# A graph-transformer layer on one core: experts' weight splits in smaller portions, own row buffers, aligned rows, and GpSimd subtracts every fourth piece

## The reference

```python
xn = _layernorm(x)
x = x + graph_layers(xn, src, dst) + linear_attention(xn)
xf = _layernorm(x)
probs = softmax(xf @ router_w);  topw, topi = top_k(probs, 2)
h = silu(einsum('nd,edf->nef', xf, w1))            # w1: 8 x 1024 x 1024
ye = einsum('nef,efd->ned', h, w2)                 # w2: 8 x 1024 x 1024
routed = einsum('ne,ned->nd', combine, ye)
shared = sigmoid(xf @ shared_gate_w) * ((silu(gate) * up) @ shared_down)
out = x + routed + shared
```

## Time and profile before

| | |
|---|---|
| median of 3 runs | 1055.58 us (1055.2 to 1055.6) |
| the profiled execution's own time | 1056.61 us |
| its span, first to last instruction | 1054.6 us |
| mean granted TensorE clock | 0.996 of full speed |
| PE busy | 1032.0 us (98%) |
| VectorE busy | 649.6 us (62%) |
| ScalarE busy | 459.5 us (44%) |
| GpSimd busy | 79.1 us (8%) |

### The profile page before, as it was taken

One profiled execution on the slowest core, in us unless ns is written; L12 is line 12 of the kernel. 1 busy time (PEld: TensorE's weight loads), 2 busy tenths in 40 slices (PEclk: granted clock), 3 DMA queues, 4 the chain that ended last, 5 costly groups with the idle time before them and its releaser, 6 DMA issues.

```text
span 1054.6 us, 16055 instructions
## 1 busy us (share of the span) xinstructions
PE 1032.0 (98%) x6128; PEld 908.3 (86%) x6128; DVE 649.6 (62%) x962; ACT 459.5 (44%) x731; POOL 79.1 (8%) x123
## 2 busy tenths in 40 slices
PE   7999999999999999999999999999999999999998
PEld 5889998787787899978878999988979788998977
DVE  6789968667655765324356362244867678776546
ACT  4413344547777423220232422223666566655440
POOL 6000010000000000000000035000100010000003
PEclk9999999999999999999999999999999999999999
DMA  9722112123321222341200544233886897686618
GB/s 354 303 80 73 49 41 80 41 80 128 101 70 41 81 80 81 136 158 64 80 1 1 178 151 96 100 131 130 282 299 235 310 315 237 252 297 227 240 38 294
DMA packets 76694, 156.44 MB, mean 148 GB/s; under 512 B 8489, under 2 KB 8987, under 8 KB 76618
## 3 DMA queue, kind: packets, MB, share of 16 engines
q1 hardware_dynamic: 65656, 127.30, 34.9%
q0 software_dynamic: 6416, 20.00, 5.5%
q10 hardware_dynamic: 4546, 8.10, 2.1%
HBM read 133.89 MB, written 21.49 MB: 147 GB/s over the span
## 4 chain that ended last, share of the span: by engine, by line
PE 82%; DVE 7%; ACT 4%; DVEq 2%; DMA 2%; issue 1%; POOL 1%; ACTq 0%; POOLq 0%; SPq 0%
PE ps L1982 20%; PE ps L1984 20%; PE ps L1983 20%; PE ps L2446 5%; PE ps L2447 2%; PE ps L2471 2%; DVE w_lo L1188 2%; PE ps L2081 1%; PE ps L2313 1%; PE ps L2314 1%; PE ps L2244 1%; PE ps L2245 1%; PE ps L2095 1%; DMA y_first<-expert_rows,slots 1%; PE ps L2472 1%
## 5 line engine op out<-in xcount | busy, mean ns | idle before, releaser
L1194 DVE TENSOR_TENSOR w_lo<-w_raw,w_hi 128x2048 fp32r<-128x2048 f32 x41 | 93.1, 2288 | 38.5 <-ACT w_hi L800 36.4
L2446 PE MATMUL ps<-xe,w_hi 128*128 128x304 f32 (+2 forms) x384 | 107.6, 356 | 0.0
L1982 PE MATMUL ps<-w_hi,xt_hi 128*128 128x512 f32 (+1 forms) x240 | 96.0, 400 | 3.9 <-DVEq L1504 2.0
L800 ACT CAST w_hi<-w_raw 128x2048 fp32r<-128x2048 f32 x41 | 77.1, 1908 | 45.1 <-PE ps L2314 36.2
L2447 PE MATMUL ps<-xe,w_lo 128*128 128x152 f32 (+2 forms) x384 | 94.8, 247 | 0.0
L1188 DVE TENSOR_TENSOR w_lo<-w_raw,w_hi 128x1024 fp32r<-128x1024 f32 x68 | 78.7, 1220 | 24.5 <-ACT w_hi L796 23.9
L1984 PE MATMUL ps<-w_hi,xt_lo 128*128 128x512 f32 (+1 forms) x240 | 93.7, 390 | 0.0
L1983 PE MATMUL ps<-w_lo,xt_hi 128*128 128x512 f32 (+1 forms) x240 | 93.5, 390 | 0.0
L1188 DVE TENSOR_TENSOR w_lo<-w_late,w_hi 128x1024 fp32r<-128x1024 f32 x64 | 74.1, 1219 | 20.4 <-ACT w_hi L796 19.2
L1982 PE MATMUL ps<-xt_hi,w_hi 128*128 128x314 f32 x256 | 79.4, 310 | 0.0
L1982 PE MATMUL ps<-t_hi,w_hi 128*128 128x314 f32 x256 | 78.8, 308 | 0.0
(11 more groups left out here) (371 smaller groups left out, 2375.8 us busy)
## 6 DMA issues: line engine op xcount, KB each, us to landing
w_raw<-in_L_ffn_w SPq DMA_DIRECT2D x64, 512.0 KB, 5.4
w_late<-in_L_ffn_w SPq DMA_DIRECT2D x64, 512.0 KB, 5.8
w_raw<-in_L_gnn_W_neigh SPq DMA_DIRECT2D x8, 1024.0 KB, 6.1
w_raw<-in_L_gnn_W_self SPq DMA_DIRECT2D x8, 1024.0 KB, 5.1
w_raw<-in_L_ffn_shared_gate_up SPq DMA_DIRECT2D x8, 1024.0 KB, 6.2
expert_rows<-ctx_s POOLq DMA_DIRECT2D x15, 512.0 KB, 13.3
w_raw<-in_L_mix_Wv SPq DMA_DIRECT2D x4, 1024.0 KB, 14.8
w_raw<-in_L_mix_Wk SPq DMA_DIRECT2D x4, 1024.0 KB, 5.3
```

Of the source, the lines that this page charges most:

```text
L800: copy(w_hi[b][:, s * HK:(s + 1) * HK, :], w_raw[s][:, :, :]).then_inc(hi_done, 1)
L1194: V_.tensor_tensor(w_lo[b][:, k, :], w_raw[s][:, :, :], as32(w_hi[b][:, k, :]), ALU.subtract).then_inc(lo_done, 1)
L1982: mat(out_ap, lh, rh, start=start, stop=False)
L2446: mat(PS(key)[:, a, 0:2 * width], wh[:, k, w_cols], xe[:, :, k, 0:width], start=k == 0, stop=False)
```

## The change

Four things at once.

1. **GpSimd subtracts.** The last of the four pieces of every job of the experts is subtracted by GpSimd (`last_lo`), in its queue between the gathers; DVE does three. It counts on a semaphore of its own, for which PE and SP wait (`wait_lo`). Each gather of the next expert's rows now stands behind the subtraction for the present expert's first job.
2. **Split portions.** ACT and DVE no longer do a whole job at a time while they make the hidden values: the first piece of a job goes ahead of the SiLU of units n = 1 and n = 3, the rest behind it. In a ONE expert the cast of job J+2 goes ahead of the rows of the expert before, and the transposes of the next expert's last tile go behind the first `y` unit. Turned outputs `yf` use two buffers in place of four; the reduction of `yf` 2 waits until the first two have been turned back.
3. **Own row buffers.** In a ONE expert, which has one tile of rows, the two halves go to two buffers in place of one.
4. **Aligned rows.** `BS` is 256, so that each block of `xe` and `he` is 1024 bytes; `at_hi` and `q_first` start 64 bytes lower. The late buffer of the fourth piece moves to a place that is free by then.

```diff
-    B, BS = 224, 224
+    B, BS = 224, 256
...
-            return [("ht", q, 0)] + following[:2] + [("ht", q, 1)] + following[2:] + y_units(q)
+            return [("ht", q, 0)] + following[:2] + [("ht", q, 1)] + y_units(q)[:1] + following[2:] + y_units(q)[1:]
...
-        at_hi = at("at_hi", RG, [128, KF, TQ], f32r)
+        at_hi = at("at_hi", RG - RG % 512, [128, KF, TQ], f32r)
...
+        row_buffer = lambda q, h, s: h if ONE[q] else s
...
+            def last_lo(job, base=None):
+
+                pool.wait_ge(hi_done, by(count_at(job, PARTS - 1), base, 4 * PARTS))
+                k = slice((PARTS - 1) * PK, PARTS * PK)
+                nc.gpsimd.tensor_tensor(w_lo[job % 2][:, k, :], raw_part(job, PARTS - 1), as32(w_hi[job % 2][:, k, :]),
+                                        ALU.subtract).then_inc(last_lo_done, 1)
...
+            last_lo(J_X)
+            for q in range(FIXED):
+                pool.wait_ge(lo_out, rows_in[q])
+                if q + 1 < FIXED:
+                    gather_rows(q + 1)
+                else:
+                    gather_block(slice(0, 1))
+                for job in range(J_X + 4 * q + 1, J_X + 4 * q + 5):
+                    last_lo(job)
...
# ACT, hidden values of a turned or two-tile expert
+                split_hi(job + 1, j)
+                for n in range(KF // 2):
+                    in_s = he_s[:, n % 2, :, 0:width]
+                    if n % 2:
+                        split_hi(job + 2 + n // 2, j, pieces=(0,))
+                    act.wait_ge(he_added, by(sums[q] + n + 1, j, KF // 2))
...
+                    if n == 1:
+                        split_hi(job + 2, j, pieces=range(1, PARTS))
...
# DVE, the same
+                    V_.reduce_sum(in_s, both_parts(key, width), axis=AX.X).then_inc(he_added, 1)
+                    V_.drain().then_inc(free[slot(key)], 1)
+                    split_lo(job + 1 + (n + 1) // 2, j, pieces=(0,) if n % 2 else (PARTS - 1,))
+                    dve.wait_ge(hi_out, by(nth[key], j, BR))
+                    V_.tensor_tensor(two(he_lo), in_s, as32(two(he_hi)), ALU.subtract).then_inc(lo_out, 1)
+                    if n == 1:
+                        split_lo(job + 2, j, pieces=range(1, PARTS - 1))
```

More of the change, by code:

```diff
@@ L563, in gps_layer @@
         gathered = [16 * sum(len(rows) for rows in ROWS_OF[:q + 1]) for q in range(AGAIN + 1)]
-        stores = [[32 * sum(len(rows) > s for rows in ROWS_OF[:q]) for s in range(BC)] for q in range(LOOP + 1)]
+        row_buffer = lambda q, h, s: h if ONE[q] else s
+        stores = [[sum(16 if one else 32 for one in ONE[:q]) for s in range(BC)] for q in range(LOOP + 1)]
         copies = [sum(2 * len(rows) for rows in ROWS_OF[:q]) for q in range(LOOP + 1)]
@@ L766, in _ @@
                 gather_block(bass.ds(j + 1, 1))
+                for job in range(J_LOOP + 1, J_LOOP + 5):
+                    last_lo(job, j)
             pool.wait_ge(xg_loaded, blocks * (16 * BC) + gathered[LOOP])
@@ L793, in split_hi @@
                 if job >= J_X:
-                    for s in range(PARTS):
+                    for s in pieces:
                         act.wait_ge(part_loaded[(job - J_X) % 2][s], by(16 * ((job - J_X) // 2 + 1), base, 32))
@@ L1156, in expert @@
                 for h in range(2):
-                    split_hi(job + 2 + h + 1, j)
+                    split_hi(job + 3 + h, j, pieces=range(PARTS) if h or ONE[q] else range(1, PARTS))
                     for s, rows in enumerate(ROWS_OF[q]):
                         out_rows(q, h, s, j)
-                        if h == s == 0 and not ONE[q]:
+                        if h == s == 0:
                             for later in xe_units(q + 1)[2:]:
@@ L1179, in _, with split_lo @@
             V_ = nc.vector
-            def split_lo(job, base=None, quarters=(0, 1)):
+            def split_lo(job, base=None, quarters=(0, 1), pieces=range(PARTS)):
                 b = job % 2
                 if job >= J_X:
-                    for s in range(PARTS):
+                    for s in pieces:
+                        if s == PARTS - 1:
+                            continue
                         dve.wait_ge(hi_done, by(count_at(job, s), base, 4 * PARTS))
@@ L1867, in hidden_features @@
                 job, width = J_X + 4 * q, sum(ROWS_OF[q])
[L1868 to L1878, removed]
+                split_lo(job + 1, j, pieces=range(PARTS - 1))
+                for n in range(KF // 2):
+                    key = ("he", q, n)
+                    in_s = he_s[:, n % 2, :, 0:width]
+                    two = lambda t: t[:, 2 * n:2 * n + 2, 0:width]
+                    wait_unit(key, j)
+                    V_.reduce_sum(in_s, both_parts(key, width), axis=AX.X).then_inc(he_added, 1)
[5 more added lines that the diff above has]
+                        split_lo(job + 2, j, pieces=range(1, PARTS - 1))
             def features_out(q, n):
@@ L1889, in turned_out @@
                 job = J_X + 4 * q
-                split_lo(job + 3)
+                split_lo(job + 3, pieces=range(1, PARTS))
                 features_out(q, 0)
@@ L1914, in expert @@
                     hidden_across(q, 1)
-                else:
-                    split_lo(job + 3, j)
+                split_lo(job + 3, j, pieces=range(PARTS) if ONE[q] else range(1, PARTS))
                 for key in xe_units(q + 1)[2:]:
                     rows_lo(key, j)
-                if ONE[q]:
-                    split_lo(job + 3)
                 split_lo(job + 4, j)
```

85 lines of the change are left out of this document (42 added, 43 removed).

## The result

The changed kernel takes 1049.2 us (median of 4 runs, 1048.05 to 1050.92) where the kernel before took 1055.4: 0.9943 of it, interval 0.9926 to 0.996, 6.2 us less. The forecast was 1044.3. The profiled execution took 1050.92 us, its span is 1048.8.

What follows compares the result with a forecast made beforehand. PE, busy 98% of the span, bounds the kernel. Terms -2.8 - 3.2 - 3.6 - 3.2 + 1.5 = -11.3 us took the median 1055.58 to 1044.3 us; range 1041.5 to 1046.5, or 1041 to 1050 with rivals.

Steps and rivals of the forecast that it cites:

- portions, row buffers: In the turned experts, PE's waits for the reductions of `yf` and `he` go: -3.6 us.
- alignment: Matmuls with `at_hi`, `he` or `xe` stationary take 5 ns less each, over 720 matmuls: -3.2 us, ends 0 and 4.4.
- ONE order and clock: In q = 1 and q = 3, first `y` units begin sooner (-2.8 us) and both half-rate windows go (-3.2 us).
- sum without GpSimd: All gains of the change together, before the new waits for GpSimd's subtraction: 12.8 us.
- GpSimd's piece: GpSimd's subtraction takes 2.4 us; new PE waits of 0.7 us before q = 2, 0.8 before q = 4: +1.5 us.
- the rivals: Clock still halves (0.15), VectorE and GpSimd collide (0.13), alignment does nothing (0.08); with these three, 1041 to 1050 us.
- Rival (b): DVE and GpSimd hold each other up: turned experts' 3.6 us stay, two critical places 0.6 later each; 1049.1 us, chance 0.13.
- Order: ONE experts: first `y` unit begins 2.23 us sooner in q = 1, 1.74 in q = 3, less 1.2 for transposes: -2.8 us.
- Clock: ONE experts q = 1 and q = 3: both half-rate windows vanish, -3.2 us, with zero as the other end.
- Turned experts: PE's waits of 2.3 us for reductions of `yf` and 1.3 us for `he` go: -3.6 us.

## Why the prediction was right and wrong

Taken in the order portions, alignment, order, GpSimd, the medians make a ladder. A step is a difference of two medians, each known to 1.5 us (the changed kernel's to 1.8), so the steps of 2.6 and 3.8 us are the least sure.

| step | forecast | measured | from, to (us) |
|---|---|---|---|
| portions, row buffers | -3.6 | -6.9 | 1055.4, 1048.5 |
| alignment | -3.2 | -2.6 | 1048.5, 1045.9 |
| ONE order and clock | -2.8 - 3.2 | -3.8 | 1045.9, 1042.1 |
| sum without GpSimd | -12.8 | -13.3 | 1055.4, 1042.1 |
| GpSimd's piece | +1.5 | +7.0 | 1042.1, 1049.2 |

**The step that failed is GpSimd's piece.** Its length was right: I took 2.4 us, and alone it takes 2.39. What was wrong is "a new wait of 0.7 us before q = 2" and, by the same count, 0.8 before q = 4. That count let VectorE's three subtractions take what they always take. They took 5.67 us in place of 3.50, PE waited 2.2 and 1.7 us, and I left out that a wait of that size in the experts can bring a half-rate window of its own, though the earlier trace rows show one behind a stretch with waits. 3.9 + 3.4 = 7.3 us is the measured cost within the noise. 1049.2 lies outside the forecast's own 1041.5 to 1046.5 and inside the 1041 to 1050 that holds only with the rivals. (The upper end of the former, by its own terms, is 1044.3 + 0.9 + 1.6 = 1046.8.)

**Rival (b) had the mechanism, and its figure of 1049.1 us is right by accident.** It let the 3.6 us of the turned experts stay and gave 0.6 us to each critical place. The runs show the opposite: the reductions read PSUM and are not held up, so those waits go, and each critical place costs about 3.6 us (half of 3.9 + 3.4). I gave it 0.13 because nothing in the trace spoke for it; nothing in the trace could, since POOL hardly worked beside VectorE's subtractions. The absence of a row is no evidence against a collision.

The Trainium skill (SBUF — State Buffer, "Who interferes with whom") says that a VectorE instruction with two SBUF inputs contends with a GpSimd instruction that reads SBUF and not with one that only writes it, and that the second to issue blocks until the first is done. The rows agree in all three: VectorE's third subtraction takes 3.40 us behind GpSimd's subtraction, 2.06 behind its copy and 1.22 beside its memset. The Trainium skill (GPSIMD Engine Reference, section 3.1) gave 1.96 times VectorE's time; this case shows 2.39 / 1.22 = 1.96. With the 1.16 us that the prediction took for a piece on VectorE, 1.96 times would have been 2.3.

**Order.** Right in its places: the first `y` unit of q = 1 starts 2.13 us after the second SiLU (770.92 to 773.05; forecast 2.1), and counted from PE's first transposes of `he_t` (771.47 before, 770.34 now) it is 2.15 us sooner (forecast 2.23), in q = 3 1.7 (1.74). **Clock** was half right. Both windows leave the ONE experts, but the changed kernel has two others behind the new waits, and without GpSimd the term is mis-sized: once the portions and the alignment are in, the old order has one window in its profile and not always two, so order and clock together are worth 3.8 and not 6.0 us.

**Turned experts.** The waits went, as forecast, and the term was too small: 3.6 us was what the list of waits shows, and the window above shows another 0.84 us in q = 4 alone that the list does not hold, time inside matmuls counted as busy around the waits. PE's unit starts put 0.3 us in q = 0 and 1.7 in q = 5; when the shared expert's last product begins 5.7 us are gained (1022.09 to 1016.39). The rest of the 6.9 lies in the tail and was not taken apart.

**Alignment.** Right, 3.2 forecast, 2.6 and 3.0 measured in two settings.

**Where they meet.** The order and GpSimd's piece get in each other's way. With the old order the piece costs 3.3 us (1045.9 to 1049.15), with the new one 7.0; the order earns 3.8 us without GpSimd and nothing beside it. A likely reason: the new order has VectorE split the rows of the next expert between ACT's first cast of job J+4 and its own first subtraction, so a hold-up one job earlier turns into a second one.

The best version is the change without its GpSimd part: 1042.1 us, 13.3 less than before and 7.0 less than the kernel as changed.

## What to carry to other kernels

Work given to GpSimd beside VectorE is not parallel where GpSimd reads SBUF and VectorE's instruction has two SBUF inputs: count the sum of both lengths on VectorE's list wherever GpSimd's can start first, and price the relief by the waits that it ends. Here it was 3.5 us on the kernel before, where PE waited for VectorE's reductions, and nothing once smaller portions had ended the same waits. If the work must be shared, let GpSimd begin behind VectorE's last instruction of the batch; one wait earned 5.0 us here. When a sum takes a wait into account on an engine at 98%, give the sum with and without a half-rate stretch behind it.

## What the runs showed of the hardware

- GpSimd's subtraction of 128x1024 fp32 takes 2.39 us alone and 2.25 from the end of the VectorE instruction in front of it, its copy 0.9 in the same count and its memset 0.95; VectorE's subtraction takes 1.22, and 3.40 and 2.06 when the first or the second of these is ahead of it. Reductions out of PSUM beside a GpSimd piece kept their 0.79 us.
- GpSimd's own instruction grows as well when it comes second: 2.86 us where it started 0.6 us before VectorE's third subtraction had ended. The two end 2.23 to 2.28 us apart in all but one of the 31 pieces of the changed kernel that begin beside a VectorE subtraction, so most of these rows of 2.4 to 3.1 us are one length of some 2.25 us and a wait.
- A stationary operand whose blocks do not all start at multiples of 512 bytes relative to `xt_hi` costs 4 to 7 ns a matmul of 512 columns (medians of 393 to 396 against 389), 2.6 to 3.0 us over this kernel. Whether a smaller multiple would do was not tried.
- A half-rate window (granted clock 0.50, the 1.2 of 1.2 and 2.4 GHz, 3.4 us long) costs 1.7 us. In the profiled executions one stood behind PE's wait of 2.2 us, and none behind waits of 1.72, 1.0 and 0.9 us in kernels that had no longer one. In the kernel before they stood behind shorter ones around transposes, the longest of 1.22 us in q = 1 and three of 0.4 us in q = 3, and none behind 1.29 us in q = 4. What exactly brings one is open.
